# Folding Wo times W1 on the chip, and a float32 down product, in the expert FFN at the end of a one-core layer

## The reference, cut to what matters

```
y  = scan(...)                       # 2048 tokens x 64 numbers
x3 = y @ Wo + bo                     # Wo 64 x 256
route = sigmoid(x3 @ Wr + br); e = argmax(route); prob = max(route)      # one of 8 experts per token
h  = gelu(x3 @ W1[e])                # W1[e] 256 x 1024, exact gelu
out = x2 + prob * (h @ W2[e])        # W2[e] 1024 x 256
```

## Time and profile before

| what | value |
|---|---|
| runs (median) | 794.11, 794.45, 796.13 us (794.45) |
| profiled execution, span first to last instruction | 793.7 us |
| left around the span, against the median | 0.75 us |
| mean granted clock of the core | 0.994 |
| PE busy | 771.0 us, 97%, 4438 instructions |
| DVE busy | 477.7 us, 60% |
| ACT busy | 521.8 us, 66% |
| POOL busy | 251.1 us, 32% |
| first up product of the tile loop starts | 620.24 us |
| last down product released the last `o_tile` | 785.46 us |

### The profile page before, as it was taken

One profiled execution on the slowest core, in us unless ns is written; L12 is line 12 of the kernel. 1 busy time (PEld: TensorE's weight loads), 2 busy tenths in 40 slices (PEclk: granted clock), 3 DMA queues, 4 the chain that ended last, 5 costly groups with the idle time before them and its releaser, 6 DMA issues.

```text
span 793.7 us, 13176 instructions
## 1 busy us (share of the span) xinstructions
PE 771.0 (97%) x4438; PEld 510.2 (64%) x4438; DVE 477.7 (60%) x859; ACT 521.8 (66%) x700; POOL 251.1 (32%) x310
## 2 busy tenths in 40 slices
PE   8999999999999999999999999999999899999994
PEld 5778888887777887533332332332655688888884
DVE  5887776639866763284331211211458699999994
ACT  4432222455233226799999999999466688888882
POOL 6444544314433421410000000100000477666652
PEclk9999999999999999999999999999999999999998
DMA  8241111101133704032752531500593681111000
GB/s 245 41 82 43 38 53 53 54 1 53 35 122 111 174 12 81 1 60 75 133 152 35 80 60 21 81 2 1 193 324 119 228 283 54 51 55 37 25 12 0
DMA packets 52762, 64.99 MB, mean 82 GB/s; under 512 B 15969, under 2 KB 44009, under 8 KB 52716
## 3 DMA queue, kind: packets, MB, share of 16 engines
q1 hardware_dynamic: 44580, 55.96, 27.5%
q0 software_dynamic: 3312, 6.31, 2.6%
q10 hardware_dynamic: 4824, 2.12, 1.0%
HBM read 51.52 MB, written 15.60 MB: 85 GB/s over the span
## 4 chain that ended last, share of the span: by engine, by line
PE 57%; ACT 20%; DVE 11%; issue 9%; DVEq 1%; DMA 1%; ACTq 1%; POOLq 0%; SPq 0%
PE psum L1676 40%; ACT pexp L848 15%; PE psum L1781 5%; PE psum L1768 4%; DVE w_lo L1546 3%; PE psum L1869 2%; ACT w_hi L1025 2%; PE psum L2060 2%; DVE hl L1084 1%; DVE hh L1232 1%; ACT w_hi L1030 1%; DVE ssum L1272 1%; DMA x_tm<-in_x 1%; DVEq L476 1%; DVE w_lo L1541 1%
## 5 line engine op out<-in xcount | busy, mean ns | idle before, releaser
L848 ACT ACTIVATE pexp<-psum 128x1024 f32<-128x1024 f32 x256 | 236.5, 1135 | 2.7 <-PE psum L1768 2.6
L835 ACT ACTIVATE hid<-psum,b_col 128x512 f32<-128x512 f32 x96 | 66.1, 688 | 163.1 <-PE psum L1676 123.1
L1781 PE MATMUL psum<-pexp,v_ones 128*32 128x512 f32 x1024 | 136.2, 605 | 0.4 <-ACT pexp L848 0.4
L1768 PEld LDWEIGHTS psum<-q_stack,k_stack 48*128 48x128 f32 x512 | 44.1, 184 | 114.6 <-ACT pexp L848 103.4
L1084 DVE SCALAR_TENSOR_TENSOR hl<-hid,scale_col,hh 128x341 fp32r<-128x341 f32 x192 | 104.7, 587 | 3.4
L1768 PE MATMUL psum<-q_stack,k_stack 48*128 48x512 f32 x512 | 106.2, 471 | 0.0
L1232 DVE TENSOR_SCALAR hh<-hid,scale_col 128x341 fp32r<-128x341 f32 x192 | 71.0, 411 | 57.5 <-ACT hid L835 40.2
L1358 DVE COPY yT<-psum 128x512 f32<-128x512 f32 x16 | 11.1, 691 | 122.8 <-PE psum L1781 122.8
L1676 PE MATMUL psum<-hh,w2h 128*128 128x512 f32 x192 | 76.6, 399 | 1.8 <-DVE hl L1084 1.7
L1676 PE MATMUL psum<-x_hi,w1h 128*128 128x512 f32 x192 | 77.0, 401 | 0.6 <-DVE x_lo L1098 0.6
L1676 PE MATMUL psum<-hh,w2l 128*128 128x512 f32 x192 | 75.0, 391 | 0.0
(11 more groups left out here) (286 smaller groups left out, 1436.3 us busy)
## 6 DMA issues: line engine op xcount, KB each, us to landing
w_all<-in_L_ffn_W SPq DMA_DIRECT2D x16, 1024.0 KB, 7.9
raw<-in_L_cond_ew SPq DMA_DIRECT2D x32, 256.0 KB, 3.2
parts_d<-parts SPq DMA_DIRECT2D x8, 1024.0 KB, 4.1
q_stack<-parts_d SPq DMA_DIRECT2D x48, 128.0 KB, 4.3
k_stack<-parts_d SPq DMA_DIRECT2D x48, 128.0 KB, 6.9
raw<-in_L_cond_sw SPq DMA_DIRECT2D x16, 256.0 KB, 3.7
x_tm<-in_x SPq DMA_DIRECT2D x4, 512.0 KB, 7.5
x_d<-x_tm SPq DMA_DIRECT2D x2, 1024.0 KB, 11.3
```

The lines of the kernel that those rows point to most:

```text
L835: act.activation(hid[k % 4][:], bank(k % 4), ACT.Gelu_apprx_tanh, bias=b1_col[:, bass.ds(4 * q + k // 2, 1)]).then_inc(gelu_done, 1)
L848: act.activation(pexp[mt % 2][:, 2 * j:2 * j + 2, 512 * h:512 * h + 512], psum[:, 2 * r:2 * r + 2, :], ACT.Exp, scale=D ** -0.5)\
L1768: ins = pe.matmul(psum[:, 2 * r + lane, :], k_stack[i][rows, j, mt * P:(mt + 1) * P], q_stack[i][rows, j, 512 * h:512 * h + 512], start=Tr ...
L1781: ins = pe.matmul(psum[VW * j:VW * j + VW, 6 + h, :], v_ones[i][:, mt, j, :], pexp[mt % 2][:, j, 512 * h:512 * h + 512], start=(mt == 0), ...
```

## The change

The up product no longer uses x3 and W1. Before the loop and during its first tiles the kernel computes for each expert the 64 x 1024 matrix Wo @ W1[e] and the row bo @ W1[e] (`fold`, plain float32, twelve of them: eight matrices and four bias folds of two experts each). Each fold goes from PSUM over ACT (`copy_fold`) to POOL, which splits it (`split_fold`), and SP moves the parts by DMA from SBUF to their rows in `t_all` (`move_fold`). The gathered row now holds x2 (256), and y twice (2 x 64), so that one gather of 384 numbers replaces two of 256 and one transpose gives y twice. The up product is two products for each half: the stacked high and low part of the matrix against y's high part twice, and the matrix's high part with the two bias rows against y's low part and two rows of ones. The down product is one plain float32 product per contraction step, on W2 as it was loaded; ACT and DVE only copy the transposed gelu output, one half each. PE reads each tile's expert into a register itself, and all tile loops are unrolled. x3, its store and `keep_warm` are gone; y is turned (`turn_rows`), copied twice and stored instead.

The core of the diff:

```diff
+ROW = C + 2 * N
+FOLDS = [("bias", 0), ("fold", 0), ("fold", 1), ("bias", 2), ("fold", 2), ("fold", 3),
+         ("bias", 4), ("fold", 4), ("fold", 5), ("bias", 6), ("fold", 6), ("fold", 7)]
+FIRST_FOLDS = 8
+XS = 4
+        def moves(k):
+            return 16 * sum(8 if FOLDS[j][0] == "bias" else 4 for j in range(k % 2, k + 1, 2))
...
 # sync (SP)
+                if g == 6:
+                    sp.wait_ge(normed, 8)
+                    for e in range(3):
+                        load_w1(e)
...
+            def move_fold(k):
+                what, e = FOLDS[k]
+                sp.wait_ge(fold_split, k + 1)
+                if what == "bias" and e != 2:
+                    sp.wait_ge(folded, FOLDS.index(("fold", e + 1 if e else 0)) + 1)
+                high, low = fold_hi[k % 2], fold_lo[k % 2]
+                if what == "fold":
+                    for h in range(2):
+                        sp.dma_start(t_all[half[0], RE - 1 - e, :, h, :].bitcast(F32),
+                                     wide(high[half[h], :].bitcast(F32), 1, 2)).then_inc(fold_moved[k % 2], 16)
+                        sp.dma_start(t_all[half[1], RE - 1 - e, 0, h, :].bitcast(F32),
+                                     low[half[h], :].bitcast(F32)).then_inc(fold_moved[k % 2], 16)
+                else:
+                    for j in range(4):
+                        for row, part in ((N, high), (N + 1, low)):
+                            sp.dma_start(t_all[row:row + 1, RE - 1 - e - j // 2, 1, j % 2, :].bitcast(F32),
+                                         part[32 * j:32 * j + 1, :].bitcast(F32)).then_inc(fold_moved[k % 2], 16)
+            for k in range(FIRST_FOLDS - 2):
+                move_fold(k)
+                if k % 3 == 2:
+                    load_w2(k // 3 + 1)
...
 # gpsimd (POOL)
+            def split_fold(k):
+                i = k % 2
+                pool.wait_ge(fold_out, k + 1)
+                if k >= 2:
+                    pool.wait_ge(fold_moved[i], moves(k - 2))
+                pool.tensor_copy(fold_hi[i][:], fold_raw[i][:]).then_inc(fold_high, 1)
+                pool.wait_ge(fold_high, k + 1)
+                pool.tensor_tensor(fold_lo[i][:], fold_raw[i][:], fold_hi[i][:].bitcast(F32), ALU.subtract)\
+                    .then_inc(fold_split, 1)
+            for i in range(XS):
+                pool.memset(xs[i][:], 0.0).then_inc(rows_base, 1)
+            for k in range(FIRST_FOLDS - 2):
+                split_fold(k)
...
+            for s in range(XS):
+                load_rows(s)
+            for k in range(FIRST_FOLDS - 2, FIRST_FOLDS + 1):
+                split_fold(k)
             for s in range(TILES):
                 pool.wait_ge(fo_out, s + 1)
+                if s + XS < TILES:
+                    load_rows(s + XS)
...             # scatter as before
+                if FIRST_FOLDS + 1 + s < len(FOLDS):
+                    split_fold(FIRST_FOLDS + 1 + s)
 # scalar (ACT)
+            def copy_fold(k):
+                act.wait_ge(folded, k + 1)
+                after(act, fold_split, k - 1)
+                act.copy(fold_raw[k % 2][:], bank(fold_bank(k))).then_inc(fold_out, 1)
+            copy_fold(0)
             act.activation(act_warm[:], ones[0:1, 0:1], ACT.Sigmoid)
+            copy_rows(0)
             act.wait_ge(logits_out, 1)
             act.activation(route[:], route[:], ACT.Sigmoid).then_inc(route_done, 1)
+            store_rows(0)
+            copy_rows(1)
+            store_rows(1)
+            for k in range(1, FIRST_FOLDS - 2):
+                copy_fold(k)
...
 # tensor (PE)
+            def fold(k):
...
+                for c in range(CK):
+                    if what == "bias":
+                        for j in range(4):
+                            ins = pe.matmul(psum[32 * j:32 * j + 32, fold_bank(k), :], bo_wide[:, c, 0:32],
+                                            w1_raw[e + j // 2][:, c, 512 * (j % 2):512 * (j % 2) + 512], ...)
+                    else:
+                        for h in range(2):
+                            ins = pe.matmul(psum[half[h], fold_bank(k), :], woT[:, c, half[h]],
+                                            w1_raw[e][:, c, 512 * h:512 * h + 512], ...)
+            fold(0); make_logits(0); turn_rows(0); fold(1); make_logits(1); turn_rows(1); fold(2)
+            rank(); fold(3); fold(4); fold(5)           # then the token and probability products
+            fold(6); fold(7)
...
+            for s in range(TILES):
+                if s + 2 < TILES:
+                    places.append(place_of_expert(pe, s + 2))
+                down(s, 0, places[s])
+                if s + 2 < TILES:
+                    turn_x(s + 2)
+                if FIRST_FOLDS + s < len(FOLDS):
+                    fold(FIRST_FOLDS + s)
+                if s + 1 < TILES:
+                    turn_h(s + 1, 0)
+                down(s, 1, places[s])
+                if s + 1 < TILES:
+                    turn_h(s + 1, 1)
+                if s + 2 < TILES:
+                    up(s + 2, places[s + 2])
```

More of the change, by code:

```diff
@@ L415, in layer_kernel @@
         rows_base = sem("rows_base")
-        x2s_in = [sem(f"x2s_in{i}") for i in range(2)]
         out_stored = [sem(f"out_stored{i}") for i in range(2)]
@@ L630, in _ @@
+            for k in range(len(FOLDS) - 2, len(FOLDS)):
+                sp.wait_ge(fold_moved[k % 2], moves(k))
+            load_w2(7)
             sp.wait_ge(x2_stored, 16 * NB)
@@ L2008, in _ @@
             rank()
-            pe.wait_ge(tanh_done, 2)
-            bias_x3(2)
-            make_x3(2)
-            pe.wait_ge(x3_out, 2)
-            bias_x3(3)
-            make_x3(3)
-            keep_warm(2)
-            pe.wait_ge(x3_out, 4)
+            for k in range(3, 6):
+                fold(k)
             pe.wait_ge(token_hot, 1)
@@ L2048, in expert_up, with turn_x, up @@
-            def expert_up(s, i):
+            for k in range(6, FIRST_FOLDS):
+                fold(k)
+            def turn_x(s):
+                pe.wait_ge(xs_in[s % XS], 16 * (s // XS + 1))
+                after(pe, x_lo_out, s - 1)
+                after(pe, fo_out, s - 2)
+                pe.transpose(turned_row(s), xs[s % XS][:, C:], ident[:]).then_inc(xs_turned, 1)
+            def up(s, place):
+                if s < RE:
+                    for k, (what, e) in enumerate(FOLDS):
+                        if (what == "fold" and e == s) or (what == "bias" and e == s - s % 2):
+                            pe.wait_ge(fold_moved[k % 2], moves(k))
@@ L2099, in _, with down @@
-            expert_down(0, 0)
-            with pe.Fori(0, (TILES - 3) // 2) as m:
-                tile(2 * m + 1, 1, m + 2)
-                tile(2 * m + 2, 0, m + 3)
-            turn_h(TILES - 2, 1)
-            expert_up(TILES - 1, 0)
-            expert_down(TILES - 2, 1, between=lambda: turn_h(TILES - 1, 0))
-            expert_down(TILES - 1, 0)
+            def down(s, q, place):
+                if q == 0:
+                    after(pe, fo_out, s - 1)
+                    if s < RE:
+                        pe.wait_ge(w2_in[s], 16)
+                pe.wait_ge(second_turned if q else first_turned, s + 1)
+                for f in range(4 * q, 4 * q + 4):
+                    w2 = w2_all[:, bass.ds(place, 1), C * f:C * f + C].rearrange("p e n -> p (e n)")
+                    ins = pe.matmul(out_bank(s), fhT[s % 2][:, f, :], w2, start=(f == 0), stop=(f == FC - 1))
+                ins.then_inc(w2_used, 1)
```

498 lines of the change are left out of this document (188 added, 310 removed).

## The result

The changed kernel takes 791.27 us (median of seven runs, 789.07 to 793.18) against 794.45 for the kernel before (also seven runs by now, 794.11 to 796.13): ratio 0.9953, 95% interval 0.994 to 0.9967. It is faster, by 3 us and not by the 20 that were forecast. The profiled execution took 789.91 with a span of 788.1, at a mean granted clock of 0.979. By spans, 788.1 against the forecast 773.0, 15.1 us are missing.

The account below looks back on a forecast made before the run. PE was taken to bound the loop, DVE's weight split right behind. First down product 633.4, loop 131.4 and end 8.2 gave a 773.0 us span, with 0.75 about 774 (chance 0.50); own range 768 to 780, wider range 765 to 788.

Parts of the forecast that it names:

- The loop's four terms: PE's work per tile: down 3.46, up 0.92, transposes 0.87, turned row 0.13, together 5.38 us.
- The 0.12 for registers: Added to each loop tile for PE reading operands through a register, making 5.5 us; 2.6 over 22 tiles.
- C: Rival: PE's register loads show at tile heads, 0.63 us exposed in 21 tiles, 13 us: 787; chance 0.11.
- E: Rival: PE's program never gets ahead, each tile pays register load and arithmetic, 7.2 us a tile: 811; chance 0.07.
- rival B: Cheaper way in: splits at 1.65, shorter landings, perhaps no register cost: 774 less some 6, 768; chance 0.20.
- the 1.0 us for the folds inside the loop: Allowance in the loop's 131.4 us for a late gather of tile 7, POOL standing in `split_fold(11)`.
- rival D: Chain of folds also holds the loop at `up(6)`, with landings of 4.3 and splits of 2.7: 784; chance 0.12.
- SP's issue: Each fold move issued in 0.46 us with its wait: a bias fold's eight take 3.7, a matrix's four 1.85.
- Landings: Fold moves land after 2.4 us, between 2.4 from below and 4.3 from above.
- The chain to the first gather: Splits 0 to 5, each waiting for the move two before, put the first gather at 623.5, 8.5 us later.
- From gather to transpose: On the way into the loop, 3.06 us from first gather to first transpose, as before: 626.6.
- The clock: Low for some 4 us around 630, so the first two up products take twice 0.92, say 1.75 each.

Follow-up runs that it names:

- e1: Changed kernel with the gathers of tiles 0 and 1 issued after four splits instead of six, those of tiles 2 and 3 after six: 780.29 us, ratio 0.9800.
- e10: Changed kernel with three buffers of each kind for the folds instead of two, all orders kept: 779.85 us, ratio 0.9795.
- e11: Changed kernel with gathers ahead of late splits, three fold buffers, and half of the late bias moves on ACT's queue: 774.60 us, ratio 0.9729.
- e12: e11 with the down product as three fp32r products on high and low parts: 773.31 us, ratio 0.9711.
- e3: Kernel before the change with only the down half of it, a plain float32 down product: 800.68 us, ratio 1.0066.
- e4: Changed kernel with 13 unused products filling PE's idle time ahead of the loop: 788.89 us, ratio 0.9935.
- e7: Changed kernel with W2 of experts 1 and 2 loaded ahead of all fold moves: 791.63 us, ratio 0.9953.
- e5: Changed kernel without the bias folds, keeping 66 rows of y's low part, with larger low-part moves (not a candidate): 778.39 us, ratio 0.9789.
- e2: Changed kernel without the bias folds and their moves, with 64 rows of y's low part (not a candidate): 790.11 us, ratio 0.9941.

## Why the prediction was wrong

By spans, the first down product is at 642.06 and not at 633.4 (8.7 late), the loop from there to the last output is 139.7 and not 131.4 (8.3), and the end behind it is 6.3 and not 8.2 (1.9 less): 15.1. The time of 791.27 lies above the range of 765 to 788; that it is faster came out as forecast, by 3 us of 20. The end is 6.3 in e1, e10, e11 and e12 too and 8.2 in e3, so it came with the up half of the change; why is not shown. The forecast did not have it, and misses by less for it.

**The loop's four terms: right.** Up 0.94 for 0.92, down 3.46 as taken, transposes and turned row 0.98 for 1.00. The 0.12 for registers was not needed: 5.38, not 5.5, and rivals C and E, which had PE pay for its register loads, are refuted by a PE without a gap and by e3. Half of rival B's reason (no register cost) held, and none of its result. ACT, at 38%, is above the third that was given as a sign. Two readings were off and small: DVE's rows for before were added up to 7.1 a tile, where the window has 6.6, and a fold was taken at 1.75 from two calls of 3.63 together; it measures 1.87.

**The steps that failed** are two. One is the way into the loop: the first gather was put at 623.5 and its landing at 3.06, and they measured 628.24 and 5.05. The other is the 1.0 us for the folds inside the loop, where some 6 to 8 were lost: the wait at `up(6)` and that for the rows of tile 4 stood in the sum at nothing. The mechanism of the first, splits that wait for moves, was named, and its sizes were wrong. Of the second only the wait at `up(6)` was named, as rival D.

**SP's issue: mis-sized.** Taken 0.46 from the earlier trace rows, which are loads from DRAM of 128 KB each and no moves within SBUF; measured 0.59 for a bias row and 0.61 to 0.70 for a matrix part, with one of about 1.1 in every eight. Bias fold 0 took 5.8 us (605.05 to 610.81) and not 3.7, and fold 3 (619.40 to 624.82) 5.4; a matrix 2.8 and not 1.85.

**Landings: mis-sized, both ways.** Taken 2.4 for all moves, since they were "far smaller" than those of the earlier trace rows. That holds for a bias row (2 KB) and not for half a matrix, which is 128 to 256 KB as in those rows. Measured 1.7 to 2.0 for a bias row, 3.6 to 3.8 for a matrix half (medians). On the sum ahead of the first gather they nearly cancel; the issues do not. The Trainium skill, DMA: Bandwidth & Descriptors (Anatomy of one DMA), has some 2.0 us fixed and the bytes on top, in a section on DMAs that GpSimd issues; these are SP's. The trace agrees for the bias rows (1.7 to 2.0); the matrix halves took 1.6 to 1.8 more than the fixed part.

**The chain to the first gather** ran at the forecast's steps: late by 3.1 at the end of fold 1's moves, 3.6 at their landing, 4.0 at the end of split 3, 5.7 at the end of its moves, 4.5 at their landing, 4.7 at the gather: 628.24 for 623.5. Of this 1.9 are older than the change's chain: the first fold starts at 598.59 and not at 596.7, after a wait of 3.32 for x at 9.5 us (before: 1.31 at 8.5). In e1, e4 and e10 it starts at 597.4 to 597.6.

**From gather to transpose: wrong.** Taken 3.06 as before; measured 5.05 (and 4.9 to 7.2 over the first gathers). This step was a quantity that I carried over from before, where little else was in flight (DMA share 0.23 in the earlier trace rows; after, 1.05 from 632 to 636). That the traffic makes it late is argued and not shown by a single edit: e7 took W2's first loads from behind the moves, but the share stayed at 0.94 and the landing 5.1. Across the kernels the first gather's landing follows the DMA share between its issue and its landing: 3.0 us at 0.15 (before, smaller rows), 3.4 at 0.40 (e10), 4.7 at 0.79 (e1), 4.9 at 1.01 (after), 5.2 at 0.96 (e7), and 9.4 at 1.05 in e5, whose moves are larger. The rows of the last five are of one size. The rest of the entry: the second transpose came 2.2 behind the first and not 1.6, from it to the first up product it was 1.0 more than taken (of it 0.7 waiting for y's low part), and from the up products to the down product 0.4 more at the low clock: together 2.0+0.6+1.0+0.4, which with 4.7 is the 8.7.

**The clock: the place right, the length not.** I had it low for 4 us around 630. It was 0.50 from 620 to 628 already, while PE ran the products of the probabilities and bias fold 6, and 0.50 to 0.51 from 632 to 640, in the up products. PE had been idle for 2.17 us up to 616.3, which I had not forecast: DVE's `tile_hot` came late (below). e4 puts the price of the second stretch at about 1 us.

**The folds in the loop: rival D, larger.** I allowed 1.0 for a late gather of tile 7. It was late (681.89) and cost nothing, since PE stood at `up(6)` meanwhile. Measured: 3.4 at tile 4, since its gather stood behind split 8, which waited 14.41 us for the moves of bias fold 6, and this gather then took 7.75; 1.5 on the fold product at the low clock (3.40 for 1.87; I had a fold at 1.75); 2.8 at `up(6)`, against the sign that no `up(4)` to `up(7)` waits for moves; some 2 on the products behind it. Less the 2.6 for registers and the 1.0 allowed, that is some 6 of the 8.3; about 2 are not assigned. D had the place, `up(6)`, and the wait of bias moves for PE's folds, with landings of 4.3 and splits of 2.7. The splits took 2.0 to 2.3; what made the wait was the issue price behind PE's last fold, and at tile 4 the order on POOL. Its 784 is still 7 short, since I priced it on `up(6)` alone and never looked at what queues behind a waiting split: the gather of tile 4. I did write that POOL stands in `split_fold(11)`, and did not ask the same of splits 8 to 10.

**Shown by experiments:** splits ahead of gathers cost 12 us by medians (e1; 7 at the entry in the traces), as does having two buffers (e10); these overlap, and with either the entry is within 1 us of the forecast. With three buffers, the gather ahead of the split and a second queue for moves (e11) the first down product is at 633.88 (forecast 633.4), the loop 132.1 us (131.4) and the end 6.3 (8.2): a span of 772.3, against the 773.0 forecast, that the shorter end helps to meet. So the loop's sum is in reach once the moves are out of the way.

**The distance between span and time** was taken at 0.75. The profiled executions of after, e1 and e3 took 1.8 more than their own spans, and after's median lies 3.2 above its profiled span: 2.4 us of the 17.5 between 773.8 and the median are this term.

## What to carry to other kernels

Here the loop of an edit that frees the busy engines could be worked out well from rows; what ate the gain was the new chain of small transfers that feeds it. Price each issue on its queue by a transfer of its own form, count those of one buffer's round trip, ask what the issuing queue itself waits for (here PE's last fold), and for each wait in an in-order queue ask what stands behind it: here a gather. With two buffers and a round trip longer than the work per piece, try a third buffer first: it gave 12 us here. And take a change apart by halves: the down half cost 5 us alone (e3) and is even where the up half is in (e11 against e12).

## What the runs showed of the hardware

- **Weights of 64 rows.** Products alternating between 128 and 64 contraction rows went at 0.43 each, between 128 and 66 at 0.23 (e2, after): dropping two rows cost 0.76 us a tile, and 12 us over the kernel (e2 against e5, though e5's moves are larger and its gathers later). Why is not shown.
- **DVE held by POOL.** The subtraction on POOL takes 1.29 us, and DVE instructions issued beside it stretch: one of 128x8 at 610.16 took 1.13 (0.17 in before), one of 128x16 at 612.90 took 1.14 (0.17), `tile_hot` at 618.17 took 1.62 (0.55):

```profile
609.98 1.29 POOL L752 TENSOR_TENSOR fold_lo<-fold_raw,fold_hi 128x512 fp32r<-128x512 f32 x1
```

```profile
610.16 1.13 DVE L1485 TENSOR_TENSOR re<-re,re 128x8 f32<-128x8 f32 x1
```

  DVE's instruction ends with POOL's (611.29 and 611.27). The Trainium skill, SBUF — State Buffer (Who interferes with whom), has a VectorE instruction with two inputs in SBUF contend with a GpSimd one that reads SBUF, and the one that comes second wait. The trace agrees, and shows which one paid: I had put it on the splits (2.7 each); those ahead of the first gather took 2.0 to 2.3, and DVE's routing was late by it.
- **PE reading through registers** costs nothing to be seen: with two sets of register-addressed products a tile (up and down), PE had 20.00 us of work in 20, and the tile is the sum of its products.
- **An issue on SP's queue** of a move within SBUF took 0.59 us for a row of 2 KB and 0.61 to 0.70 for half a matrix, with one of about 1.1 in eight; the loads of the earlier trace rows took 0.44.
- **A gather of 128 rows** landed after 3.4 us at a DMA share of 0.40 (e10) and after 9.4 at 1.05 (e5).
